# Four chained cross-attention layers: every maximum is added to the queries by VectorE, at a later place in its order

## The reference

```python
q, k, v = x @ Wq, ctx @ Wk, ctx @ Wv
p = softmax(q @ k.T / sqrt(8))
x = (p @ v) @ Wout + bout + x
```

## Time and profile before

| | |
|---|---|
| median of 3 runs | 2125.64 us (2123.58 to 2131.87) |
| the profiled execution's own time | 2122.2 us |
| its span, first to last instruction | 2120.4 us |
| granted TensorE clock over the span | 0.979 |
| PE busy | 2026.3 us (96%) |
| PEld busy | 1741.2 us (82%) |
| DVE busy | 1488.0 us (70%) |
| ACT busy | 1110.1 us (52%) |
| POOL busy | 461.7 us (22%) |
| chain that ended last | PE 93%, issue 3%, DVE 2%, DMA 1% |

### The profile page before, as it was taken

The page is one execution under the profiler, slowest core; times in us unless marked ns, Lnnn a source line. Parts: engine busy times, 40 slices in busy tenths (PEclk is TensorE's granted clock), DMA queues, the critical chain, the costliest instruction groups (busy, mean ns, idle before and its releaser), DMA issues.

```text
span 2120.4 us, 76562 instructions
## 1 busy us (share of the span) xinstructions
PE 2026.3 (96%) x26906; PEld 1741.2 (82%) x26906; DVE 1488.0 (70%) x4466; ACT 1110.1 (52%) x2907; POOL 461.7 (22%) x872
## 2 busy tenths in 40 slices
PE   4899999999999999999999999999999999999975
PEld 3688888888888888888888888888888888888764
DVE  3367777776777777767767777777777777777754
ACT  1355555555555555555555555555555555555431
POOL 1122222122122222212212222222221222222110
PEclk9999999999999999999999999999999999999976
DMA  4211111211111111121111111211211111121000
GB/s 115 60 39 50 54 47 44 55 46 49 49 48 51 49 53 47 44 53 49 42 55 48 49 49 46 54 45 49 53 43 55 47 44 54 47 55 27 24 9 5
DMA packets 107495, 101.00 MB, mean 48 GB/s; under 512 B 41880, under 2 KB 83872, under 8 KB 107104
## 3 DMA queue, kind: packets, MB, share of 16 engines
q1 hardware_dynamic: 105888, 94.37, 16.3%
q10 hardware_dynamic: 1216, 1.47, 0.2%
HBM read 34.13 MB, written 5.41 MB: 19 GB/s over the span
## 4 chain that ended last, share of the span: by engine, by line
PE 93%; issue 3%; DVE 2%; DMA 1%; ACT 0%; ACTq 0%; SPq 0%; POOLq 0%; DVEq 0%; POOL 0%
PE ps_s L780 13%; PE ps_c L858 12%; PE ps_s L814 9%; PE ps_c L925 8%; PE ps_k L682 6%; PE ps_k L878 6%; PE ps_q L759 5%; PE ps_c L914 5%; PE ps_s L830 5%; PE ps_k L707 5%; PE ps_k L883 4%; PE ps_c L891 4%; PE ps_c L930 3%; PE ps_k L710 2%; PE ps_q L844 2%
## 5 line engine op out<-in xcount | busy, mean ns | idle before, releaser
L1187 DVE TENSOR_REDUCE top<-ps_s 128x6 f32<-128x462 f32 (+3 forms) x1024 | 512.0, 544 | 69.2 <-PE ps_s L780 63.9
L1075 ACT ACTIVATE p_t<-ps_s 116x512 f32<-116x512 f32 (+1 forms) x768 | 375.4, 544 | 76.7 <-PE ps_s L814 70.9
L780 PE MATMUL ps_s<-k_blocks,q_sb 32*128 32x231 f32 (+1 forms) x3584 | 319.8, 380 | 19.0 <-issue 17.1
L858 PE MATMUL ps_c<-p_t,v_rows 116*27 116x128 f32 (+1 forms) x7168 | 280.5, 278 | 7.9 <-DMA v_rows<-v_img 3.7
L1418 POOL TENSOR_TENSOR k_blocks<-k_sb,mask_k 128x231 f32<-128x231 f32 x384 | 212.5, 575 | 260.3 <-PE ps_s L814 236.3
L780 PEld LDWEIGHTS ps_s<-k_blocks,q_sb 32*128 32x128 f32 x3584 | 215.9, 184 | 62.6 <-issue 26.5
L1227 DVE TENSOR_TENSOR weighted<-ps_k,probs 128x462 f32<-128x462 f32 (+1 forms) x256 | 142.2, 556 | 167.5 <-PE ps_k L883 165.7
L858 PEld LDWEIGHTS ps_c<-p_t,v_rows 116*27 116x27 f32 (+1 forms) x7168 | 209.1, 106 | 43.1 <-issue 16.5
L1103 ACT ACTIVATE o_t<-ps_c 128x256 f32<-128x256 f32 x256 | 98.4, 384 | 254.7 <-PE ps_c L914 189.4
L814 PE MATMUL ps_s<-q_sb,k_blocks 32*116 32x128 f32 (+1 forms) x5376 | 221.1, 283 | 8.7 <-DVE probs L1202 8.2
L1427 POOL TENSOR_TENSOR weighted<-weighted 128x720 f32<-128x720 f32 x64 | 93.0, 1453 | 604.9 <-DVE weighted L1227 604.9
(11 more groups left out here) (118 smaller groups left out, 3654.4 us busy)
## 6 DMA issues: line engine op xcount, KB each, us to landing
v_rows<-v_img SPq DMA_DIRECT2D x128, 227.4 KB
context<-in_ctx SPq DMA_DIRECT2D x64, 336.0 KB, 3.0
q_sb<-top_t SPq DMA_DIRECT2D x522, 6.0 KB
v_rows<-v_img SPq DMA_DIRECT2D x64, 115.2 KB
v_rows<-v_img SPq DMA_DIRECT2D x64, 112.2 KB
v_rep<-v_dram SPq DMA_DIRECT2D x64, 50.0 KB
gram<-g_img SPq DMA_DIRECT2D x64, 46.3 KB
q_sb<-top_t SPq DMA_DIRECT2D x174, 2.0 KB
```

The source lines that it names most:

```text
L780: ins = pe.matmul(ps_s[:, z * 512 + j * GT:z * 512 + j * GT + n], q_sb[c % 3][lo:lo + QUAD, j * S:(j + 1) * S], k_blocks[c % 3][lo:lo + QU ...
L858: ins = pe.matmul(ps_c[t % 2][32 * (g % 4):32 * (g % 4) + UC, g // 4 * S:(g // 4 + 1) * S], v_rows[b % NC][0:n, v:v + UC], p_t[c % 3][0:n, ...
L1075: act.activation(to, source, ACT.Exp, scale=SCALE).then_inc(p_ready, 1)
L1187: dve.tensor_reduce(top_at(c, z), s.rearrange("p (h t) -> p h t", t=T)[:, :, 0:n], AX.X, ALU.max).then_inc(s_top, 1)
```

## The change

`MOVED` becomes (0, 0), so that `moved(c)` is never true: `tops` and `move_top` are never issued, TensorE never waits for `top_ready`, and `add_top` is issued for all 192 units of the first three layers. And `add_top` goes to another place in VectorE's order: from just behind the reductions to behind `image_branch(k, t - 5, 3, 8)`, ahead of `new_x`. In kind 0 that is behind image steps 3 to 7, in kind 1 behind image steps 19 and 20, the weights and the first `weigh`, in kind 2 behind the first `weigh`.

```diff
-MOVED = (16, 248)
+MOVED = (0, 0)
@@ step of VectorE
                         top_of(k, t, i)
                         if ip(t):
                             less_top(k, t, i)
-                if added(t):
-                    add_top(k, t)
                 if ip(t - 6):
                     image_branch(k, t - 6, 19, 21)
                     image_weights(k, t - 6)
...
                     image_branch(k, t - 4, 1, 3)
                 if ip(t - 5):
                     image_branch(k, t - 5, 3, 8)
+                if added(t):
+                    add_top(k, t)
                 if out(t) and not ip(out_step(t)):
                     new_x(k, t)
```

## The result

| | before | after |
|---|---|---|
| median of 4 runs each, same chip | 2128.76 us (2123.58 to 2132.19) | 2148.16 us (2142.75 to 2154.43) |
| ratio | | 1.0105, 95% interval 1.0074 to 1.0136 |
| the profiled execution's own time | 2122.2 us | 2142.75 us |
| its span | 2120.4 us | 2140.9 us |

A forecast was written before the change was run, and what follows sets the result against it. TensorE bounds, following VectorE at kind 1's transposition; 21.6 + 2.7 + 0.2 - 2.4 = +22 us on 2122.2 gives 2144, put at 2146 us towards the runs' median. Range 2129 to 2160, the forecast's own 2140 to 2152, chance 0.58.

The forecast's parts named there:

- What bounds the kernel: TensorE, busy 96%; only kind 1's transposition ends on VectorE, which hides up to 0.09 us of wait there.
- What is removed: 174 ScalarE copies of 0.28 us and 696 SyncE DMA issues of 0.74 us; gain taken as 0.
- Kinds 1 and 2: 116 additions of 0.42 us fit VectorE's idle time: cost 0; uncovered, 0.34 us per step.
- Kind 0: Addition starts late, GpSimd holds image steps 10 and 11, kind 1's transposition is late by 0.48 us (other end 0.22).
- (a): Kind 0: addition starts after 0.03 us, no collision on step 10; 0.22 us per group, +8 us, about 2133; chance 0.17.
- 45 groups: Loop groups that begin no pass: 0.48 us late each, +21.6 us.
- 9 groups that begin a pass: VectorE is already late by 0.3 us there, covering part: 0.3 us each (0.05 to 0.48), +2.7 us.
- 3 groups behind the loop: Straight code with the early start and no held transposition: +0.2 us together.
- the last two groups with the addition at the old place: Addition moves behind image steps 3 to 7: 8.09 us becomes 6.9, giving back 1.2 us twice, -2.4 us.
- (b): Something else holds the loop's transposition, so VectorE's 0.48 us falls into a gap: -2.4 us, about 2123; chance 0.10.
- (d): Added register work delays VectorE's queue, or late results make TensorE wait at turn_out: 13 us more, about 2160; chance 0.09.
- (c): Faster: image steps 12 and 13 start clear of GpSimd, results no later than 1002.28: 7 to 15 us gained; chance 0.06.

The follow-up runs named there:

- the place alone: Kernel after with MOVED back at (16, 248), so only units at both ends are added, at the new place: 2121.51 us, 0.9976 of before.
- the swapped waits: Kernel after, with add_top waiting for q_evac first and for the transposition (top_psum) second: 2139.61 us, 1.0067 of before.
- the written mark: Kernel after, with GpSimd's L1406 a fill that reads no SBUF, behind a product of 2 columns that carries the wait: 2145.65 us, 1.0086 of before.
- the addition behind step 11: Kernel after, with kind 0's addition moved behind new_x and image steps 8 to 11, ahead of results: 2119.45 us, 0.9966 of before.
- both waits in order: Kernel after, with kind 0's addition behind image step 11, add_top's waits swapped and TensorE's turn_top waiting for reductions last: 2121.24 us, 0.9972 of before.

## Why the prediction was right, and where it wasn't

**What bounds the kernel: right.** Only kind 0's stretch ends on VectorE, and it follows VectorE one to one: L1298 is late by 0.47 us (3.86 instead of 3.39 behind the transposition), and the next transposition by the same 0.47.

**What is removed, at 0: right within what can be told.** With 116 copies fewer the kernel is not measurably different from the one with the place alone (2121.68 and 2121.51 us, beside 2126.88 and 2126.55 of before).

**Kinds 1 and 2, at 0: right but for one group in six.** The stretches from kind 1 to 2 took 433.5 against 434.2 us, and the run with only those added has kind 0's stretch unchanged in 36 of 45 groups; in the other 9 it is 0.31 longer, of which below.

**Kind 0, at 0.48 us: right, link by link.** Expected and seen, behind the kind 0 transposition's start: addition 0.44 and 0.45, L1295 of 0.32 and 0.32, L1290 of 0.50 and 0.50, results 2.86 and 2.85, L1298 3.87 and 3.86, next transposition 7.33 and 7.32. That it hung on the start of the addition is shown by the swapped waits (7.07, rival (a)'s figure); that GpSimd held the two steps, by the written mark. The reason that I gave for the late start, a second wait whose target must first be computed, fits the swap (with the early wait first, its computing lies ahead of the transposition's end), and fits that the swap gains 0.09 us only where targets are computed and loses 0.06 where they are constants. The swap shows the order of the waits to be the cause; what happens inside no trace shows.

**Sizes.** The sum had +22, and the two profiled executions differ by 20.5 us; its parts:

| term | forecast | measured |
|---|---|---|
| 45 groups | +21.6 | +23.1 |
| 9 groups that begin a pass | +2.7 | +3.0 |
| 3 groups behind the loop | +0.2 | +0.4 |
| the last two groups with the addition at the old place | -2.4 | -2.4 (33.61 to 32.38, 8.09 to 6.87) |
| kinds 1 and 2, from kind 2 on | 0 | +4.1 (-0.7 and +4.7) |
| behind unit 257 | 0 | -8.3 |
| up to the loop | 0 | +0.6 |

The first four terms hold: +24.0 where 22.1 stood. The first is 1.5 us short because of one group in six, whose stretch is 7.56 instead of 7.32 us: 9 x 0.24 = 2.2 us; against that, each group is late by 0.46 or 0.47 and not 0.48. VectorE's timeline there (transposition at 857.78):

```profile
861.42 0.18 DVE L1295 SCALAR_TENSOR_TENSOR rs_y<-rs_u,rs_y 128x24 f32<-128x24 f32 x1
861.87 0.24 DVE L1298 TENSOR_TENSOR z_b<-z_a,rs_y 128x80 f32<-128x80 f32 x1 [0.27 <-DVE rs_y L1295]
```

Between two operations that stand 0.22 us apart elsewhere lies 0.45 us, at the same place of each pass, put down to a result that had long been there. Nothing that I ran explains it. It is at the same group of the pass with the swapped waits (7.30), with the mark written (7.33 and 7.54), with kinds 1 and 2 added (7.16, there 0.21 us ahead of a reduction) and at the place of before (8.52); before the change and with the addition behind step 11 the stretch doesn't show it. With kind 0 alone added that group has 7.32, and the next one 7.42, with 0.12 us idle ahead of L1311. So it comes and goes with which additions stand in the loop, those of kinds 1 and 2 too, and my 0 for them is wrong by it.

The last three rows of the table were not foreseen, and they nearly cancel (-3.6 us): that the sum came within 1.5 us of the two executions' difference is luck, and the 24.0 where 22.1 stood is what the working is worth. Behind unit 257 there are more additions, which I had counted as unchanged: straight code at the old place paid there too. One stretch of it is shown above (1.17 us). For the rest, 258's turn to 262's, before has 30.8 to 33.4 us in three executions and the kernels with the new place 27.7 to 30.9; they overlap, so I can't tell how much of the 5.7 us is the kernel's. From kind 2 on, the growth lies at the restarts of the loop, 17.7 to 18.5 us before and 17.8 to 19.7 after. At each long one the granted clock is at the lower level (1.2 GHz), as for most of this window of after, whose mean is 0.57:

```profile
535.00:539.00 4.00, 3.68 (x32) 3.22 (x36) 2.06 (x5) 0.39 (x2) 0.00 (x0) 0.57 0.51 138
```

Each such restart costs some 1.5 us, and after has three (19.67, 19.52, 19.48 us): nearly the whole +4.7. Executions of before had 0, 6.8 and 3.4 us of the lower level within the loop, those of after 10.2 and 13.7, the one with all additions at the old place 34.1 (at seven of its eight restarts, two of them with twice the time, which makes its 15 us, and once from kind 1 to 2). The swapped waits have 17.1, kind 0 alone and the written mark 23.9 each, the place alone 6.8, kinds 1 and 2 alone 3.4; but the fast kernel with the addition behind step 11 has 10.2 too, and the one with both waits in order, whose stretches are the shortest, 17.1. TensorE is idle at every restart, with a fall or without: for 1.8 to 2.6 us in the first execution of before, which has none, and for 2.0 to 2.3 at the three of after that have one. So more waiting may bring more of it, and I leave open whether it does; it is also why a forecast of this kernel from one execution can't be better than a few us.

**The rivals.** (a) is what the swapped waits made of the kernel: 12.7 us above before where it said 8. Its kind 0 stretches sum to 11.6 us more than before's (385.2 less 373.6), where (a) had 10.4; what else differs is within the few us of the restarts, five of which were long in its profiled execution. (b) falls with the 7.32 us, (d) with L914, which starts where it did. (c) said that the order could win if results started no later than before; the addition behind step 11 does that, and still wins nothing to speak of in the loop (373.2 against 373.6 us), for step 13 is held as before: its gain of 0.3% is the end's, as the place alone shows with 0.2%.

## What to carry to other kernels

An operation that is cheap by its own duration (0.34 us) is free only in a gap that stands behind the wait which opened it: ahead of that wait it made the chain late by 0.68 us, of which 0.47 reached the bounding engine; in the gap, nothing. Where another engine's operations lie close by, work out the start of each small operation against them to a few hundredths, in both orders; 0.09 us decided 0.25 here. And where targets are computed, as in the loop here, put the wait that is met early first (0.09 us sooner on VectorE, 0.04 to 0.09 on TensorE); in the straight code, where they are constants, the other order was the quicker one, by 0.06 and 0.09 us.

## What the runs showed of the hardware that I had not expected

- The order of the waits ahead of an instruction is worth time, and the better order is another in the loop than in straight code: 0.45 against 0.36 us from the transposition's start to the addition with computed targets, 0.37 against 0.43 with constant ones; and from the last reduction to TensorE's transposition 0.24 against 0.15 or 0.20 us with computed ones, 0.06 against 0.15 with constant ones.
- When VectorE's and GpSimd's operations start in the same hundredth of a us, either can win, from group to group of one execution: L1291 took 0.18 us in 21 of 45 groups and 0.61 in 24.
- An addition of 0.42 us lets the next operation on VectorE start 0.34 us behind its own start (794.34 and 794.68): in a chain it costs less than it lasts.
- An addition with one input in PSUM isn't held by a GpSimd product under way (0.42 us as ever, at the one place that can tell), where an image step with both inputs in SBUF is (0.33 instead of 0.18).
- TensorE is idle for 1.8 to 2.6 us at each restart of the hardware loop. At single restarts its granted clock then falls to the lower level, 1.5 us each, and not at the same ones in the next execution.
